# A graph-attention kernel with another cyclic order of its steps, and new hand-written orders for its first and last turns

## What is computed

```python
# layer A: masked attention, applied four times to v, then a layer norm
q, k, v = x @ Wq.T + bq, x @ Wk.T + bk, x @ Wv.T + bv
pros = softmax(where(adj == 0, -16384, einsum('bhnd,bhmd->bhnm', qh, kh)))
z = vh
for _ in range(4):
    z = 0.9 * einsum('bhnm,bhmd->bhnd', pros, z) + 0.1 * vh
x = layernorm(x + z) * gamma + beta
# layer B: a transformer block with an edge bias
nx = ln(x, ln1_g, ln1_b)
attn = softmax(q @ k.T / sqrt(32) + where(adj > 0, 0.1 * adj * adj, -inf))   # q, k, v from nx
x1 = x + (attn @ v) @ wo + bo
out = x1 + gelu(ln(x1, ln2_g, ln2_b) @ w1 + b1) @ w2 + b2                     # w1: 256 x 1024
```

## Time and profile before

| | |
|---|---|
| median of 3 runs | 2286.55 us (2285.79 to 2287.51) |
| the profiled execution | 2287.87 us, of which the span of the trace is 2286.0 us |
| granted TensorE clock, mean | 0.996 |
| DMA | 76.88 MB, mean 34 GB/s |

### The profile page before, as it was taken

One profiled execution on the slowest core, in us unless ns is written; L12 is line 12 of the kernel. 1 busy time (PEld: TensorE's weight loads), 2 busy tenths in 40 slices (PEclk: granted clock), 3 DMA queues, 4 the chain that ended last, 5 costly groups with the idle time before them and its releaser, 6 DMA issues.

```text
span 2286.0 us, 78265 instructions
## 1 busy us (share of the span) xinstructions
PE 2256.0 (99%) x29492; PEld 2148.3 (94%) x29492; DVE 1734.4 (76%) x6993; ACT 1925.5 (84%) x6478; POOL 1524.2 (67%) x1613
## 2 busy tenths in 40 slices
...
GB/s 128 19 37 32 35 39 21 39 29 31 39 25 34 39 21 39 39 21 39 33 27 39 25 34 39 22 38 39 21 39 37 23 39 26 34 39 25 32 14 20
DMA packets 95781, 76.88 MB, mean 34 GB/s; under 512 B 9648, under 2 KB 95152, under 8 KB 95408
## 3 DMA queue, kind: packets, MB, share of 16 engines
q1 hardware_dynamic: 94176, 71.73, 10.2%
...
...
## 4 chain that ended last, share of the span: by engine, by line
PE 94%; DVE 2%; ACT 2%; issue 1%; SPq 0%; DMA 0%; POOL 0%; ACTq 0%; DVEq 0%; POOLq 0%
PE ring_ps L392 41%; PE ring_ps L530 15%; PE ring_ps L474 13%; PE ring_ps L466 10%; PE score_ps L457 6%; PE ring_ps L494 5%; PE ring_ps L417 3%; ACT probs L595 1%; DVE probs L719 0%; PE ring_ps L403 0%; DVE hT_low L805 0%; DMA g_col<-in_L_gnn_ln_g_dram 0%; DVE nx L799 0%; ACT hT_high L636 0%; DVE stats L784 0%
## 5 line engine op out<-in xcount | busy, mean ns | idle before, releaser
L595 ACT ACTIVATE probs<-probs,negmax 128x128 f32<-128x128 f32 x2048 | 795.9, 396 | 10.8 <-DVE negmax L719 4.7
L877 POOL TENSOR_TENSOR probs<-probs,rinv 128x512 f32<-128x512 f32 x512 | 536.6, 1070 | 112.3 <-DVE rinv L733 112.2
L595 ACT ACTIVATION_READ_ACCUMULATOR probs<-probs,negmax 128x1 f32 x2048 | 398.3, 194 | 0.0
L616 ACT ACTIVATE zT<-ring_ps 128x512 f32<-128x512 f32 x256 | 157.4, 615 | 179.6 <-PE ring_ps L474 179.3
L392 PE MATMUL ring_ps<-inT_C_high,w_high 128*128 128x256 f32 x1024 | 300.1, 293 | 0.0
L530 PE MATMUL ring_ps<-w_high,hT_high 128*128 128x256 f32 x1024 | 296.1, 289 | 1.4 <-DVE probsT_B L744 0.9
L466 PE MATMUL ring_ps<-ident,probs 128*128 128x128 f32 x2048 | 292.9, 276 | 1.5 <-ACT hT_high L636 0.7
L530 PE MATMUL ring_ps<-w_low,hT_high 128*128 128x256 f32 x1024 | 286.4, 280 | 0.0
L530 PE MATMUL ring_ps<-w_high,hT_low 128*128 128x256 f32 x1024 | 286.2, 279 | 0.0
L392 PE MATMUL ring_ps<-inT_C_high,w_low 128*128 128x256 f32 x1024 | 283.9, 277 | 0.0
L392 PE MATMUL ring_ps<-inT_C_low,w_high 128*128 128x256 f32 x1024 | 283.8, 277 | 0.0
...
## 6 DMA issues: line engine op xcount, KB each, us to landing
...
out_dram<-x SPq DMA_DIRECT2D x128, 128.0 KB, 2.0
...
```

The lines of the kernel that those rows point to most:

```text
L595: e = act.activation(probs[:, u, h, :], probs[:, u, h, :], ACT.Exp, bias=negmax[:, u, h:h + 1], scale=-1.0, accum_out=sums[:, u, h:h + 1])
L616: act.activation(zT[k][:, :, :, :], ring(name, g).rearrange("p (b c n) -> p b c n", b=GB, c=C), ACT.Copy).then_inc(s_out[name], 1)
L877: pool.tensor_tensor(probs[:, u, hs, :], probs[:, u, hs, :], rinv[:, u, hs].unsqueeze(2).to_broadcast([P, HR, P]), ALU.mult).then_inc(s_pr ...
```

## The change

Only `ORDER`, `HEAD`, `TAIL` and the two counts of turns are other. No instruction is added or removed; every engine gets the same steps in another order, and the greatest lag is 6 in place of 5, so that there are 70 turns, of which 49 follow ORDER.

```diff
 ORDER = """
-tC/5 eB10/4 xs/1 vB/4 z0/2 h3/3 eB11/4 y0/3 u0/5 rB1/4 wA0/2 h0/2 lx/2 u1/5 lt/0 eb/3 wA1/2 u2/5 msA/1 b1/4 c0/5 n0/3
-c1/5 sA/1 i2/5 b2/5 z1/2 pB00/4 u3/5 mA00/1 laA/1 xv/2 pB10/4 mA01/1 c2/5 pB01/4 c3/5 vA/1 eA00/1 y1/3 h1/2 pB11/4
-n1/3 d0/5 eA01/1 wB0/4 z2/2 mA10/1 rA0/1 pv/4 laB/2 tB/3 mA11/1 d1/5 i0/3 eA10/1 eA11/1 h2/2 qB/3 rA1/1 wB1/4 kB/3
-pA00/1 o/4 mB00/3 y2/4 sB/3 mB01/3 g/3 z3/2 eB00/3 i1/3 pA01/1 kA/0 pA10/1 st/5 n2/4 pA11/1 msB/3 mB10/3 mB11/3 eB01/3
-qA/0 rB0/3
+pA11/2 i0/4 mB00/4 sB/4 xs/1 mB01/4 z3/3 z0/2 mB10/4 pv/5 c1/6 lt/0 b1/5 laA/0 h3/3 y0/3 h0/2 u2/6 mB11/4 u3/6 laB/3
+c2/6 st/6 c3/6 eB10/4 vA/1 eB00/4 o/5 y2/5 i2/6 sA/1 n0/3 mA00/1 n2/5 rB0/4 g/4 eb/3 mA01/1 eB01/4 wB0/5 i1/4 mA10/1
+wB1/5 wA0/2 z1/2 eA00/1 qA/0 eB11/4 msA/1 eA01/1 d0/6 d1/6 y1/3 h1/2 mA11/1 rB1/4 tC/5 b2/6 wA1/2 kA/0 eA10/1 vB/4
+rA0/1 z2/2 n1/3 pB00/4 pB01/4 pB10/4 h2/2 lx/2 tB/3 eA11/1 pB11/4 pA00/1 u0/5 qB/3 kB/3 msB/4 u1/5 xv/3 rA1/1 pA10/1
+c0/5 pA01/1
 """
...
-HEAD_TURNS = 9
+HEAD_TURNS = 11
...
-TAIL_TURNS = 8
+TAIL_TURNS = 10
...
```

More of the change, by code:

```diff
@@ L52 @@
[L52 to L76, removed]
```

90 lines of the change are left out of this document (64 added, 26 removed).

## The result

The kernel after takes 2282.41 us (median of 18 executions, 2280.50 to 2284.61) beside 2286.99 us for the kernel before on the same chip (18 executions). The ratio is 0.998, with a 95% interval of 0.9973 to 0.9986: 4.6 us faster, where 11 were forecast. The page of after has these rows; a turn can be read from two starts of sA in the timeline of PE; and the window is the same stretch as in the earlier trace rows.

A forecast was written before the change was run, and what follows sets the result against it. It took PE's own step lengths as the bound, 34.88 us a turn. Switches saved 10.8 us over 49 turns, with pace, waits and ends at zero: 2286.55 to 2275.8, rounded to 2275.5 us, range 2253 to 2293.

The forecast's parts named there:

- switches and settling of runs: On PE, three ways into scores or hops a turn instead of four save 0.22 us a turn, 10.8 us in all.
- pace: Dense matmuls on PE run at 0.113 or 0.118 us; 60 of 180 a turn stay fast, so no difference.
- waits: PE waiting for ACT, DVE or a PSUM bank in the cyclic turns; priced at nothing.
- ends: Head and tail, including SP's order of weight loads (some 2 us either way); value 0, bounds 8 us either way.
- DVE has 0.3 to 0.5 us to spare at h2 and pB11: In the seven T steps between z2 and u0, DVE's list was said to leave this room.
- The rival of the late banks: Seven T steps outrun four banks if ACT is late to z2: 0.5 us a turn, 2300 us; chance 0.12.
- hop-to-dense exit: Going in and leaving a hop straight into dense work costs 0.30 us, 0.05 more than by way of transposes.
- entry from T into scores: From transposes (pA11) into scores (sB); in no row, taken at the same cost as entry from dense work.
- D/T switches: PE switching from dense matmuls to transposes and back; both together cost 0.02 us at most.
- all-fast case: Rival: at least 110 of 180 dense matmuls fast, 0.22 us or more a turn, 2262 us; chance 0.2.
- Its rule (hops before, two T before): Dense runs on PE mostly go fast after a hop and one T step, slow after two T steps.
- The clock: Rival: clock falls from pA10 to h0, 6.1 us without dense work; 78 us lost, 2353 us; chance 0.02.

The follow-up runs named there:

- d0: The kernel of a2 plus a DVE copy of 128 columns to a spare tile ahead of pB01's read-out; 2273.9 us.
- d2: The kernel of a2 plus a DVE copy of 512 columns to a spare tile ahead of pB01's read-out; 2284.57 us.
- a1: The kernel after, with POOL's scaling of the probabilities doing only one head of four (work left out); 2246.75 us.
- a3: The kernel after, with transpose step h1 moved forward, between the two dense steps ahead of it; 2280.47 us, 0.997 of before.
- a6: The kernel of a2 with step tB moved ahead of h2 and u0 behind kB; 2306.51 us, 1.0084 of before.
- a2: The kernel after, with only DVE's norm nx moved earlier, ahead of POOL's scaling; 2253.85 us, 0.9852 of before.
- b1: The kernel before, with the load of three columns and the slow bias row moved behind w1 and its two columns; 2282.48 us, 0.9977.

## Why the prediction was wrong

Per turn and in all, forecast and measured:

| term | forecast | measured |
|---|---|---|
| switches and settling of runs | -0.22 a turn, -10.8 us | -0.32 a turn, -15.5 us |
| pace | 60 of 180 fast, 0 | 60 of 180 fast, 0 |
| waits | 0 | +0.336 a turn, +16.5 us |
| ends | 0, bounds 8 either way | -6.2 us |
| sum of the span | -10.8 us | -5.2 us |

- **The step that failed is the pricing of the waits at nothing**, and in it the sentence that DVE has 0.3 to 0.5 us to spare at h2 and pB11. The room was nearly right (0.28 by d0 to d2). What was wrong is the length of what stands ahead: the two nx, which take 0.9 us in before and 0.77 in a1 in the very place, took 1.99 beside POOL. POOL's scaling and DVE's norm were moved against each other; the forecast has SP's and POOL's room, but not what POOL and DVE do to each other's durations. The row that could have warned was in the trace of before: edges at 1223 ns for 256 columns beside norms at 406. Its sign for a wait, rows in the view of PE's waits, stayed empty in after; only the distances show it.
- **The rival of the late banks** had the place right (the seven T steps) and the engine wrong: it looked to ACT, whose list held, and gave 0.5 us a turn; it was DVE, 0.34.
- **Switches.** Without the waits the turn would be 34.565 us, 0.32 less than before. The terms hold: the hop-to-dense exit, the entry from T into scores (0.09 us, as from dense work), D/T switches free. Of the 0.1 too little, 0.03 are the seven fewer dense runs at 0.004 each, and 0.06 that a row of dense steps at 0.113 pays 0.02 until it settles (kA in before is 0.104 over its steady pace, a slow qA 0.088, u0 of after 0.081), which before did in kA, u0, u1 and u3 and after does in qA alone.
- **Pace.** The count of 60 was right, by other steps than in before, and right by luck: of the ten other kernels near it here, which have some 50 to 156 fast matmuls a turn, only a3 and a6 have about 60. The forecast's range, which took in the all-fast case at 2262 us, was the right treatment; a2 is that case, plus the wait gone. Its rule (hops before, two T before) fails: in a2 the run behind seven T steps is fast, and in d0 the one straight behind a hop slow.
- **Ends.** SP's order was named, at some 2 us; it is 5.2 by b1. The fold's wait for g_col was in the trace of before as a row with 3.05 us of idle time; in b1 two effects behind it (kA of pair 1, and a stretch of 3.2 us at half clock that no longer comes) nearly doubled it.
- **The clock.** In the stretch from pA10 to h0, 6 us without dense work, the granted clock stays at 1.00, as in the row of windows above. The rule on transposes that the forecast weighed doesn't show here either.

That the time fell inside the range (2253 to 2293) is due to two errors of opposite sign, 16.5 us lost and 10.9 won.
